# Moving one group's inner product by the cube from the seventh step's end into the eighth step

## What is computed

```python
# third layer: two graph convolutions, then LSTMs over windows of p = 1..4 nodes
h = relu(einsum('ts,bsh->bth', adj, x @ Wg0 + bg0))
h = relu(einsum('ts,bsh->bth', adj, h @ Wg1 + bg1))
for p in range(1, MAX_SKIP + 1):
    wins = h[:, :nw * p, :].reshape(Bv * nw, p, Hd)        # nw = Tv // p
    last = lstm_last(..., wins)
    h = h.at[:, arange(nw) * p + (p - 1), :].set(last)
x3 = layernorm(x2 + h)
# fourth layer: eight Euler steps, linear in h
def euler_step(h, _):
    ax = jnp.einsum('nm,bmd->bnd', adj_mx, h)
    f = alph * 0.5 * (ax - h) + h @ w_eff - h + x0
    return (h + dt * f, None)
out = layernorm(x3 + h_after_8_steps)
```

## Time and profile before

| | |
|---|---|
| median of 3 runs | 942.03 us (939.39, 942.03, 942.44) |
| the profiled execution | 940.35 us, span 938.6 us |
| mean granted TensorE clock | 0.994 of full speed |
| TensorE busy | 894.5 us, 95% of the span, 4999 matmuls |
| VectorE, ScalarE, GpSimdE busy | 72%, 60%, 35% |
| step 7's first cell to the last cell's gates | 813.42 to 880.3 us |

### The profile page before, as it was taken

One profiled execution on the slowest core, in us unless ns is written; L12 is line 12 of the kernel. 1 busy time (PEld: TensorE's weight loads), 2 busy tenths in 40 slices (PEclk: granted clock), 3 DMA queues, 4 the chain that ended last, 5 costly groups with the idle time before them and its releaser, 6 DMA issues.

```text
span 938.6 us, 14553 instructions
## 1 busy us (share of the span) xinstructions
PE 894.5 (95%) x4999; PEld 773.4 (82%) x4999; DVE 672.4 (72%) x1588; ACT 563.8 (60%) x1228; POOL 327.3 (35%) x533
## 2 busy tenths in 40 slices
PE   9799999989999899999999999999999999999996
PEld 6688887457778689989988898999889898978986
DVE  5889996676688766677667767776776777675744
ACT  5457675853674566477557737765774675476341
POOL 3665654740121422162045216303521432340121
PEclk9999999999999999999999999999999999999999
DMA  5322211211101101001201200120101001000000
GB/s 184 109 83 68 68 46 45 101 68 57 34 15 43 34 2 57 1 12 35 68 1 46 64 5 12 36 68 1 46 24 45 12 12 46 1 12 27 9 23 23
DMA packets 26595, 38.55 MB, mean 41 GB/s; under 512 B 3333, under 2 KB 12422, under 8 KB 26010
## 3 DMA queue, kind: packets, MB, share of 16 engines
q1 hardware_dynamic: 26088, 36.05, 11.6%
q10 hardware_dynamic: 434, 1.57, 0.5%
HBM read 21.89 MB, written 15.73 MB: 40 GB/s over the span
## 4 chain that ended last, share of the span: by engine, by line
PE 49%; DVE 11%; ACT 8%; POOL 7%; issue 4%; ACTq 0%; DVEq 0%; POOLq 0%
PE psum L141 14%; PE psum L143 13%; PE psum L142 13%; PE psum L1828 2%; PE psum L1829 2%; PE psum L1832 2%; ACT gate L1403 2%; POOL out_rstd L1336 1%; DVE in_h L1566 1%; ACT raw L1434 1%; POOL node_l L1354 1%; DVE x L1598 1%; ACT x L1434 1%; POOL x_rstd L1336 1%; ACT gate L1406 1%
## 5 line engine op out<-in xcount | busy, mean ns | idle before, releaser
L1403 ACT ACTIVATE gate<-psum,gate_bias 128x256 f32<-128x256 f32 (+2 forms) x296 | 143.5, 556 | 67.4 <-PE psum L1832 55.6
L141 PE MATMUL psum<-in_h,wih_h 128*128 128x256 f32 (+2 forms) x312 | 106.7, 342 | 8.8 <-DVE in_l L1570 5.0
L143 PE MATMUL psum<-in_h,wih_l 128*128 128x256 f32 (+2 forms) x312 | 103.6, 332 | 0.0
L142 PE MATMUL psum<-in_l,wih_h 128*128 128x256 f32 (+2 forms) x312 | 103.0, 330 | 0.0
L141 PEld LDWEIGHTS psum<-in_h,wih_h 128*128 128x128 f32 x312 | 59.0, 189 | 21.2 <-DVE in_l L1570 8.7
L1370 POOL TENSOR_TENSOR gate<-in_h,in_l 128x512 f32<-128x512 f32 x14 | 17.9, 1303 | 158.4 <-DVE in_l L1570 158.4
L1406 ACT ACTIVATE gate<-cell 128x512 f32<-128x512 f32 (+2 forms) x80 | 40.3, 503 | 49.6 <-DVE cell L1554 39.2
L1551 DVE TENSOR_TENSOR gate<-gate 128x256 f32<-128x256 f32 (+2 forms) x48 | 24.1, 501 | 59.7 <-ACT gate L1403 59.6
L141 PE MATMUL psum<-e_h,shared 128*128 128x384 f32 x180 | 62.1, 345 | 2.2 <-POOL e_l L1385 2.0
L142 PEld LDWEIGHTS psum<-in_l,wih_h 128*128 128x128 f32 x312 | 59.1, 189 | 5.1 <-issue 0.2
L143 PEld LDWEIGHTS psum<-in_h,wih_l 128*128 128x128 f32 x312 | 58.9, 189 | 4.6
(11 more groups left out here) (389 smaller groups left out, 2900.1 us busy)
## 6 DMA issues: line engine op xcount, KB each, us to landing
x_spill<-x SPq DMA_DIRECT2D x30, 256.0 KB, 2.0
xt<-in_x_t_dram SPq DMA_DIRECT2D x16, 256.0 KB, 2.6
raw<-x_spill SPq DMA_DIRECT2D x16, 256.0 KB, 2.9
o_spill<-xt SPq DMA_DIRECT2D x14, 256.0 KB, 2.0
xt<-o_spill SPq DMA_DIRECT2D x14, 256.0 KB, 3.4
x<-x_spill SPq DMA_DIRECT2D x14, 256.0 KB, 3.4
out_dram<-raw SPq DMA_DIRECT2D x14, 256.0 KB, 2.3
raw<-in_adj_t_dram ACTq DMA_DIRECT2D x1, 1024.0 KB, 9.0
```

The costliest lines, as they stand in the source:

```text
L141: pe.matmul(dst, lh, rh, start=start, stop=False, **kw)
L142: pe.matmul(dst, lh, rl, start=False, stop=False, **kw)
L143: return pe.matmul(dst, ll, rh, start=False, stop=stop, **kw)
L1403: nc.scalar.activation(gate[q][:, 0:n], banks[GATE_BANK[q]][:, 0:n], ACT.Tanh if q == 2 else ACT.Sigmoid, bias=gate_bias[:, p - 1, q:q + 1 ...
```

## The change

For step 6, new lists (EVE_PE, EVE_ACT, EVE_DVE) stand in place of the regular ones. They leave out the inner product of group 5 from list 10, and put the gather ahead of the second coefficients there. For step 7, the inner product of group 5 (under the names lateinner, latesum, latelow, counted among DONE_NAMES and with the same functions as before) stands in list 1. The giant product with its sum and output norm's statistics goes from list 1 to list 2, and the transpose of x3, the first power's both halves and the second power come together in list 3.

```diff
-        DONE_NAMES = ("giant", "gianta", "giantb", "ysum", "outsum", "out", "outhalf")
-
-        LAST_PE = FILL_PE[:8] + [["coefs0_1"], ["coefs1_1"], ["inner_0", "inner_1", "hturn"]]
-        LAST_ACT = FILL_ACT[:8] + [["coefs0_1"], ["coefs1_1"], ["inner_0", "inner_1"]]
-        LAST_DVE = FILL_DVE[:8] + [["coefs0_1"], ["coefs1_1"], ["innersum_0", "innerlow_0", "innersum_1", "x3add_0", "x3early_0",
-                                                               "innerlow_1", "x3add_1", "x3early_1"]]
-        LAST_POOL = FILL_POOL[:10] + [["whole", "x3early_0", "x3early_1"]]
+        DONE_NAMES = ("lateinner", "latesum", "latelow", "giant", "gianta", "giantb", "ysum", "outsum", "out", "outhalf")
+
+        EVE_PE = FILL_PE[:10] + [["gather1_1", "coefs1_1", "weight1_1", "hturn"]]
+        EVE_ACT = FILL_ACT[:10] + [["gather1_1", "coefs1_1", "input_1"]]
+        EVE_DVE = FILL_DVE[:10] + [["gather1_1", "coefs1_1", "weight1_1", "input_1", "x3add", "x3first"]]
+
+        LAST_PE = [[], ["lateinner_0", "lateinner_1"], ["giant_2", "giant_3", "giant_0", "giant_1"],
+                   ["x3t_0", "power1a_0", "power1b_0", "power2_0"]] + FILL_PE[4:8] + [
+                       ["coefs0_1"], ["coefs1_1"], ["inner_0", "inner_1", "hturn"]]
+        LAST_ACT = [[], ["x3norm_0", "lateinner_0", "x3split_0", "evens_h", "lateinner_1"], ["evens_l"],
+                    ["x3t_0", "power1_0", "power2_0", "out_0"]] + FILL_ACT[4:8] + [
+                        ["coefs0_1"], ["coefs1_1"], ["inner_0", "inner_1"]]
+        LAST_DVE = [[], ["latesum_0", "latelow_0", "latesum_1", "latelow_1"], ["x3sum_1", "ysum_1", "ysum_0", "outsum"],
+                    ["x3t_0", "power1_0", "power2_0"]] + FILL_DVE[4:8] + [
+                        ["coefs0_1"], ["coefs1_1"], ["innersum_0", "innerlow_0", "innersum_1", "x3add_0", "x3early_0",
+                                                     "innerlow_1", "x3add_1", "x3early_1"]]
+        LAST_POOL = FILL_POOL[:2] + [["x3sum_1", "outsum"]] + FILL_POOL[3:10] + [["whole", "x3early_0", "x3early_1"]]
...
-            for g in range(2, G - 1):
+            for g in range(2, G - 2):
                 step(g, cell_step, pieces, fill)
+            step(G - 2, cell_step, pieces, eve)
             step(G - 1, cell_step, pieces, last, front=False)
```

More of the change, by code:

```diff
@@ L1252, in step, with run @@
                     piece(name)
-        def run(cell_step, pieces, start, once, following, fill, last, tail):
+        def run(cell_step, pieces, start, once, following, fill, eve, last, tail):
             step(-1, None, pieces, [start], lstm=False, l3=False, done=False)
@@ L1312, in _ @@
             run(None, {"prep": prep, "ahead": prep, "norm": norm, "out": out_piece, "outhalf": out_half, "x3load": x3load},
-                START_SP, ONCE_SP, FILL_SP, FILL_SP, FILL_SP, TAIL_SP)
+                START_SP, ONCE_SP, FILL_SP, FILL_SP, FILL_SP, FILL_SP, TAIL_SP)
             for j in range(GB):
@@ L1387, in _ @@
             run(None, {"split_e": split_e, "turn": turn, "norm": norm, "x3sum": x3sum, "x3first": lambda g: x3sum(g, 0), "x3early": x3sum, "x3split": x3split, "outsum": outsum,
-                       "whole": whole_h, "clear": clear}, START_POOL, ONCE_POOL, NEXT_POOL, FILL_POOL, LAST_POOL, TAIL_POOL)
+                       "whole": whole_h, "clear": clear}, START_POOL, ONCE_POOL, NEXT_POOL, FILL_POOL, FILL_POOL, LAST_POOL, TAIL_POOL)
         @block.scalar
@@ L1529, in _ @@
                             "coefs0": lambda g, j: coefs(g, j, 0), "coefs1": lambda g, j: coefs(g, j, 1),
-                            "prep": prep, "ahead": prep, "norm": norm, "weight0": weight0, "x3norm": x3norm, "x3split": x3split, "inner": inner,
+                            "prep": prep, "ahead": prep, "norm": norm, "weight0": weight0, "x3norm": x3norm, "x3split": x3split, "inner": inner, "lateinner": inner,
                             "evens_h": lambda g: evens(g, False), "evens_l": lambda g: evens(g, True),
@@ L1534, in _ @@
                             "first": lambda t: high(0, t), "second": lambda t: high(1, t),
-                            "input": layer_input}, START_ACT, ONCE_ACT, NEXT_ACT, FILL_ACT, LAST_ACT, TAIL_ACT)
+                            "input": layer_input}, START_ACT, ONCE_ACT, NEXT_ACT, FILL_ACT, EVE_ACT, LAST_ACT, TAIL_ACT)
         @block.vector
@@ L1797, in _ @@
                             "x3low": x3low, "outhalf": out_half,
-                            "x3t": x3t, "innersum": inner_sum, "innerlow": inner_low, "ysum": ysum, "outsum": outsum,
+                            "x3t": x3t, "innersum": inner_sum, "innerlow": inner_low, "latesum": inner_sum, "latelow": inner_low, "ysum": ysum, "outsum": outsum,
                             "columns": columns, "conv_bias": conv_bias_rows, "row_sum": row_sum, "weff": weff, "bcols": spread_bias, "square": square, "cube": cube,
                             "fourth": fourth, "fc": fc, "mix": mix, "offset": offset, "lift": lift, "bias": bias, "first": lambda t: low(0, t), "second": lambda t: low(1, t),
-                            "input": layer_input}, START_DVE, ONCE_DVE, NEXT_DVE, FILL_DVE, LAST_DVE, TAIL_DVE)
+                            "input": layer_input}, START_DVE, ONCE_DVE, NEXT_DVE, FILL_DVE, EVE_DVE, LAST_DVE, TAIL_DVE)
         @block.tensor
@@ L2048, in _ @@
                             "turn": turn, "weight0": weight0, "weight1": weight1, "x3t": x3t,
-                            "inner": inner, "giant": giant, "hturn": hturn,
+                            "inner": inner, "lateinner": inner, "giant": giant, "hturn": hturn,
                             "weff": weff, "first": lambda t: product(0, t), "second": lambda t: product(1, t),
                             "square": square, "cube": cube, "fourth": fourth, "fc": fc, "offset": offset, "lift": lift, "bias": bias},
-                START_PE, ONCE_PE, NEXT_PE, FILL_PE, LAST_PE, TAIL_PE)
+                START_PE, ONCE_PE, NEXT_PE, FILL_PE, EVE_PE, LAST_PE, TAIL_PE)
 def kernel(**inputs):
```

## The result

The changed kernel takes 948.55 us (median of 4 runs, 948.17 to 948.83), the kernel before 941.69 us (median of 4). It is slower by 6.9 us. The ratio is 1.0077, 95% interval 1.006 to 1.0095, so the loss is clear of the noise; a ratio here is worked out from all runs and differs from that of the two medians by up to 0.0011. The forecast was 947.0 us.

A forecast was written before the change was run, and what follows sets the result against it. TensorE's own queue was taken to bound both places, so only its idle time counts. 4.2 us of idle time plus 1.5 for one clock fall gave 5.7, on a base of 941.3: 947.0 us, range 943.2 to 949.8.

The forecast's parts named there:

- A: The forecast case, step 7: 4.2 us of idle time and one fall of the clock, 5.7 us slower; chance 0.48.
- Part 1: Seventh step's end loses the inner products: cell 0 starts 5.7 us sooner on TensorE, its first VectorE product 4.7.
- The term for the coefficients' eviction: Seventh step's end: eviction by ScalarE and VectorE lets VectorE's sum start at about 807.35, against 809.94 before.
- the swap of gather and coefficients: Seventh step's end: neutral on TensorE, since both stand ahead of 806.21.
- Part 2: Inner product in cell 1's list, step 7: new idles of 0.5 and 2.1 us, cell 3 starts 0.7 us late.
- Part 3: Transpose and all powers in cell 3's list: 3.85 us idle ahead of the second power, cell 4 4.1 us late.
- The clock: Step 7: a fall likely behind the 3.85 us idle, 1.5 us; about 1 in 3 for another 1.5.
- Rival C: Step 7: the clock falls behind both new idles, 7.2 us slower, 948.5 us; chance 0.21.
- D: Giant product in step 7 isn't held, its inputs coming 2 us sooner: +1.6 us, 942.9 us; chance 0.09.
- E: The change fills the gap ahead of cell 4, which starts 2.1 us before its old time: 939.2 us; chance 0.05.
- The advice on interleaving regimes: Full TensorE work moved into step 7, which has gaps, would cut the time by the 2.1 us gap.

The follow-up runs named there:

- e6: Kernel before with half the first power product behind cell 3 on TensorE and the spreading casts ahead of cell 3 on ScalarE: 938.81 us, ratio 0.9992.
- e2: Changed kernel with the second power product and its read-out on ScalarE and VectorE moved behind cell 4: 947.08 us, ratio 1.0081.
- e8: e6 plus idle matmuls in the two gaps of step 1, none in step 7: 937.03 us; the same kernel run again: 936.60 us.
- e1: Kernel before with Part 3 alone: transpose, both first-power halves and second power in list 3 of step 7; 944.30 us, ratio 1.0031.
- e4: Changed kernel with Part 3 undone: transpose and first half of the first power back behind the giant product in list 2; 942.93 us, ratio 1.0025.
- e5: Kernel before with half the first power product moved from ahead of cell 3 to behind it, on TensorE alone: 940.91 us, ratio 1.0002.
- e3: Changed kernel with idle matmuls in TensorE's three gaps of step 7: 944.75 us, ratio 1.0040.

## Why the prediction was right

**Direction and method.** The time rose by 6.9 us against a forecast of 5.7. Counting TensorE's idle time between two fixed places, with the same matmuls in both kernels, gave the direction and each wait. No wait appeared that the prediction did not name. The forecast total was nevertheless partly lucky: the forecast scenario, A, had one fall of the clock, and what happened was two.

**Part 1.** Cell 0 came 6.0 us sooner from the mark, as forecast with 5.7. VectorE's first product started 811.81 less 804.57, 7.2 us behind the mark, against 12.5 before: 5.2 sooner, where 4.7 was said. The term for the coefficients' eviction was 0.4 too dear. That the swap of gather and coefficients is neutral on TensorE fits these numbers; no run tests it alone.

**Part 2.** Idle of 0.39 and 1.69 us against 0.5 and 2.1. The chain of sums and roundings that holds the giant product had the right links, ScalarE's second rounding behind the spreading casts among them. Cell 3 started 0.1 us late against 0.7.

**Part 3.** Idle of 3.73 us against 3.85, released by the named instruction. The run with part 3 alone shows it without the rest. But "the step that decides" was too strong: part 3 undone still loses 2.9 us in the profile, and part 3 alone adds 1.6 us of idle time. The idle time added by the two runs, 1.6 and 2.9 us, is 0.8 more than the change's 3.7. That is the 0.87 us ahead of the transpose in the run with part 3 undone: there it stands directly behind the giant product and waits for the output sum; behind cell 3, where part 3 puts it, this wait is gone.

**The clock.** This is the term that was mis-sized. Forecast: one fall at 1.5 us. The price of a fall of 3.4 us was right (1.5 to 1.6 from cell 7 to the end); the number and the length were not. In the profiled execution there were two, and the first lasted 6.8 us, half rate from 840.2 to 847.0, so it took in the whole second power product and cost 2.4. The second came behind cell 7's idle, which is as long as before (1.85 and 1.86) and had been taken as harmless since no fall had followed it. Filling the gaps gives 2.7 to 3.5 us for the clock in the timed runs, 3.8 in the profiled ones. The waits were 0.5 us dearer in the forecast than in the trace (4.2 against 3.7), which made up for part of it. Rival C, two falls, was nearest: it gave 948.5 us, although its second fall was placed behind the other new idle. The list of idles that the chance of a fall was read from also lacked one: TensorE is idle for 2.63 us until 37.65 in the kernel before, and the clock stays at 1.00 behind it. A third stretch at half rate in the kernel before, from about 934.3 to the end, lies behind TensorE's last matmul (929.55) and costs nothing.

**The rivals.** D (no hold ahead of the giant product) and E (the gap is filled) are out by the rows. The advice on interleaving regimes (the Trainium skill, page "Perfetto Trace Analysis", section "Optimization Strategy") did not carry here: with part 3 undone the moved work left the gap ahead of cell 4 (2.06 us) and opened three more, since in queues that run in the order written the chains that release it stood behind the cells' own.

## What to carry to other kernels

Where an engine is full up to a stretch with gaps, work moved into the stretch gains only as far as its inputs are ready inside a gap; add up the engine's idle time before and after, wait by wait. Look at the read-out that releases a product: if its instruction stands behind a long dependent chain on its own engine, move that instruction ahead of the chain, and let the product cover the chain's wait (e6). Moving the product alone to the other side of the next link only moved the idle time (e2). A gap can also cost through the clock behind it, and cheap dummy matmuls in the gap both test that and remove it.

## What was not expected of the hardware

The same gap was not always followed by the same clock. The idle of 3.22 us in step 1 stands in both kernels; behind it the clock was at half for 3.4 us in the kernel before and for 6.8 us in the one after. The idle of about 1.86 us ahead of cell 7 had a fall behind it in the changed kernel, in e2 and in e8, and none before, in e1, e4, e5, e6 and in e8's second execution; the idle of 3.10 us in e2 had none. The idle of 1.99 us in step 1 had a fall behind it in the kernel before, the changed one, e1, e3 and e5, and none in e2, e4 and e6. An idle of 2.6 us near 37 us stands in all eleven executions and had a fall behind it in six (the changed kernel, e1, e2, e4, e5 and e6). So the length of an idle alone does not say whether the clock falls, and e8 and its second execution show that one and the same kernel does both. Each fall of 3.4 us costs about 1.5 us here, so the times of one kernel spread by that and more. What decides whether the clock falls is not settled by these runs.
